# An audio tower with tree feed-forward on one core: the weighing of levels shared out, leaf numbers kept in registers, transposes and residual adds moved

## The chip, the cores and the metric

One core of one Trainium2 chip. The time is that of the kernel on the device, in microseconds; the figure for a kernel is the median of its runs. Beside the plain runs there is one profiled execution, whose own time is given with its span.

## What is computed

Four sequences of 750 rows of 128 features go through a convolution with signs of the inputs and weights (3 taps, 64 features, 748 tokens a sequence), an attention in which only the diagonal of the weights is used, and a tree feed-forward. The change touches the last part only:

```python
h = layernorm(h2)
current = 0
for i in range(8):                       # a path from the root to a leaf level
    score = h . w1s[current] + b1s[current]
    weight_i = gelu(abs(score))
    t_i = h @ w2s[current] + b2s[current]
    out += weight_i * t_i
    current = 2 * current + (score > 0) + 1
result = h2 + out
```

Each of the 2992 tokens so uses eight 64 x 64 matrices, one on each level, chosen by its own path; 128 nodes stand on the last level (the "leaves").

## The kernel before, in words

The part behind 363 us of the profile is the feed-forward. Tokens have been sorted by leaf: every leaf has a fixed group of 32 slots (the static part, 4096 slots in 32 tiles of 128), and tokens that find no room there go to overflow groups of 32 slots, which belong to one leaf each. How many overflow groups there are is known only at run time (`nact`); up to 96 are provided for, in sections of 4 tiles (16 groups) that run only under `If(groups > ...)`. For these inputs three sections are live, 12 tiles and 48 groups. GpSimd scatters the tokens' rows into DRAM (`own_slots`, L646), SP reads them back four tiles at a time into a ring of six (`load_rows`, L433), with two parts per row: the normalised features (with a one for the bias) and the residual `h2`, and the token number.

For every section of four tiles TensorE transposes the rows (`xs_T`, L995) into PSUM tile Z[0], and ScalarE copies them to SBUF (`xs_copy`, L1248, ring of three). The weight tables lie in SBUF with 65 columns a node, the last one w1, so that a product gives both `t_i` and the score. Level 0 to 3, 4 to 5, 6 and 7 are multiplied separately:

- A static tile (`tile_products`, L1016 to L1023) has fixed nodes: one product of 260 columns (4 levels) and one of 130 (2 levels) for 128 slots, two of 65 for 64 slots each, four of 65 for 32 slots each. Its result fills one of three pairs of PSUM banks (`y_bank`): the four upper levels in one bank, the four lower in the other.
- An overflow group (`overflow_products`, L1051 to L1057) has four products for 32 slots (260, 130, 65 and 65 columns) whose weights start at an address that TensorE's queue works out from a register. The leaf numbers, 7 bits each, are packed in pairs in `lami`; `load_leaves` (L1030) brings two registers, for the four groups of the next tile, between the second and the third group. For the even group of a pair each address is a shift, a mask, a multiplication and an addition, for the odd one the mask is not needed. Each group has a pair of banks of its own, and ScalarE copies it to 32 partitions of `yv` in SBUF (L1276).

Behind the products the work of a tile is a chain: ScalarE takes Abs of the eight scores (L1255) and their Gelu (L1257) to `gw`; VectorE multiplies the 8 x 64 outputs by the eight weights into `wy`, a ring of two (`weigh`, L1626), sums the eight levels into `yo`, a ring of twelve (`sum_levels`, L1634), and adds the residual (`add_residual`, L1640); GpSimd scatters the rows to the output with an indirect DMA (`rows_out`, L717). In the static part VectorE's order is weigh k, add the residual of k - 1, sum k. The order within each engine is written out by hand; semaphores tie them: TensorE reuses a pair of banks when `s_wy` says it is weighed (`bank_ready`), VectorE reuses a slot of `yo` when its transfer has landed (`s_outr`), and SP refills a slot of the rows' ring when the four tiles in it are written out. `s_goff` says that the leaf numbers and `nact` are ready.

## Time and profile before

| what | value |
|---|---|
| median of 3 runs | 499.88 us (499.46 to 502.1) |
| the profiled execution | 497.14 us, span 495.4 us |
| busy: PE, DVE, ACT, POOL | 362.6, 353.8, 297.0, 266.6 us |
| static stage, first to last weighing | 368.0 to 421.3 us |
| overflow stage, first product to last copy | 420.5 to 483.65 us |

Times in the views count from the span's start. PE is TensorE's matmul stream, PEld its weight loads, PEldq and POOLq the queues that feed the engines (register operations are not counted as busy), DVE VectorE, ACT ScalarE, POOL GpSimd. A row of the timeline merges neighbouring instructions of one kind ("x2"); in brackets stands how long the engine was idle before, and what it is held to have waited for. In the view by form a row ends with busy time, mean ns of one, and idle time before. The program names are tiles that share memory: `va` holds `xs`, `wy` and `yv`, `pre` holds `yo`, `pool_a` and `w` the weight tables, `qk` the transposed rows.

### The profile page before, as it was taken

How to read it: one execution, taken by the hardware profiler on the slowest of the kernel's cores; microseconds unless marked ns; L12 is line 12 of the kernel's file. 1: busy time of each engine (PE TensorE's matmuls, PEld its weight loads, DVE VectorE, ACT ScalarE, POOL GpSimd, SP SyncE). 2: the span in 40 equal slices, each digit the busy share in tenths (PEclk: the TensorE clock that was granted, in tenths of full speed). 3: DMA queues.
4: the chain of work that ended last, by engine and by line, in shares of the span. 5: the costliest groups of instructions: out<-in, count | busy, mean ns of one | idle time of the engine just before them, and what ended most of it. 6: DMA issues, size and time to landing. Idle time of an engine off the chain costs nothing.

```text
span 495.4 us, 8210 instructions
## 1 busy us (share of the span) xinstructions
PE 362.6 (73%) x2578; PEld 246.1 (50%) x2578; DVE 353.8 (71%) x619; ACT 297.0 (60%) x691; POOL 266.6 (54%) x354
## 2 busy tenths in 40 slices
PE   1158997767998897878987798834069887778880
PEld 1145665545555554456644475522057665545550
DVE  0558869897988888988889979776129999433341
ACT  1357987799789986777976658561013332544551
POOL 4324687885686846855896617417506555321111
PEclk9988989999999999898998989855569999999997
DMA  4443541339969722312441200197151220000000
GB/s 95 120 104 84 125 101 41 93 78 226 202 146 156 162 53 63 93 33 63 110 109 27 69 1 11 38 133 99 32 132 35 56 54 10 6 7 4 7 3 7
DMA packets 58424, 36.99 MB, mean 75 GB/s; under 512 B 31645, under 2 KB 57079, under 8 KB 58378
## 3 DMA queue, kind: packets, MB, share of 16 engines
q1 hardware_dynamic: 54250, 33.55, 33.6%
q0 software_dynamic: 3328, 2.36, 1.9%
q10 hardware_dynamic: 800, 0.49, 0.5%
q8 instruction: 26, 0.43, 0.4%
q14 instruction: 20, 0.16, 0.1%
HBM read 11.15 MB, written 7.50 MB: 38 GB/s over the span
## 4 chain that ended last, share of the span: by engine, by line
DVE 39%; PE 27%; ACT 15%; issue 11%; DMA 5%; POOL 1%; SPq 1%; DVEq 0%; POOLq 0%; ACTq 0%
DVE nm L1367 12%; ACT Z L1183 8%; PE Z L914 8%; DVE pre L1634 6%; PE Z L1051 5%; DVE va L1626 4%; DMA pre<-in_x 3%; DVE va L1396 2%; PE Z L1053 2%; ACT q L1125 2%; PE Z L1057 2%; DVE pre L1463 1%; ACT k L1125 1%; ACT va L1276 1%; PE Z L1055 1%
## 5 line engine op out<-in xcount | busy, mean ns | idle before, releaser
L1367 DVE TENSOR_REDUCE nm<-Z 125x1 f32<-125x748 f32 x192 | 175.4, 932 | 38.9 <-PE Z L914 33.2
L1183 ACT ACTIVATE Z<-Z,nm 125x748 f32<-125x748 f32 x192 | 166.1, 870 | 61.5 <-DVE nm L1367 61.2
L914 PE MATMUL Z<-pool_a 128*125 128x512 f16 (+1 forms) x768 | 164.5, 342 | 27.3 <-ACT Z L1183 23.7
L914 PEld LDWEIGHTS Z<-pool_a 128*125 128x125 f16 x768 | 88.7, 141 | 71.6 <-ACT Z L1183 45.6
L717 POOL DMA_INDIRECT out<-pre,va x44 | 42.7, 971 | 87.8 <-DVE pre L1640 78.3
L1634 DVE TENSOR_REDUCE pre<-va 128x64 f32<-128x512 f32 x44 | 45.1, 1025 | 1.3
L1276 ACT COPY va<-Z 32x520 f32<-32x520 f32 x48 | 27.9, 580 | 30.3 <-PE Z L1057 30.1
L781 PE MATMUL Z<-xhT,wq 128*128 128x249 f16 (+1 forms) x192 | 33.4, 295 | 10.5 <-DVEq L1377 9.2
L1183 ACT ACTIVATION_READ_ACCUMULATOR Z<-Z,nm 125x1 f32 x192 | 41.1, 214 | 0.0
L1051 PE MATMUL Z<-pool_a,qk 128*32 x96 | 29.6, 390 | 14.1 <-ACT va L1276 8.7
L646 POOL DMA_INDIRECT sorted_rows<-xrow,slot x24 | 30.4, 1266 | 15.3 <-DVE slot L1519 8.7
L1626 DVE TENSOR_TENSOR va<-va,gw 128x512 f32<-128x512 f32 x12 | 8.3, 691 | 38.6 <-ACT gw L1257 38.6
L614 POOL TENSOR_TENSOR va<-va 125x256 f32<-125x256 f32 (+2 forms) x54 | 29.5, 547 | 10.2 <-DVE va L1396 7.1
L1626 DVE TENSOR_TENSOR va<-Z,gw 128x512 f32<-128x512 f32 x32 | 21.7, 679 | 18.6 <-ACT gw L1257 18.4
L590 POOL TENSOR_TENSOR pool_a<-q,pool_a 128x748 f16<-128x748 f32 x15 | 24.6, 1643 | 10.2 <-DVE pool_a L1324 9.1
L781 PEld LDWEIGHTS Z<-xhT,wq 128*128 128x128 f16 x192 | 19.2, 106 | 21.1 <-DVEq L1377 13.4
L588 POOL CAST pool_a<-q 128x748 f16<-128x748 f32 x14 | 11.3, 806 | 32.2 <-ACT q L1125 32.2
L793 PEld LDWEIGHTS Z<-sel,qk 128*125 128x125 f32 x192 | 25.4, 194 | 6.0 <-DVEq L1416 1.1
L598 POOL TENSOR_TENSOR qk<-q,k 128x748 f32<-128x748 f32 x16 | 28.3, 1772 | 0.0
L1255 ACT ACTIVATE gw<-Z 128x8 f32<-128x8 f32 x32 | 5.7, 177 | 35.3 <-PE Z L1023 33.7
L793 PE MATMUL Z<-sel,qk 128*125 128x2 f32 x192 | 25.2, 236 | 1.4 <-DVEq L1416 0.9
L1016 PE MATMUL Z<-pool_a,qk 128*128 128x260 f32 x64 | 23.1, 444 | 4.1 <-DVE va L1626 4.1
(237 smaller groups left out, 620.9 us busy)
## 6 DMA issues: line engine op xcount, KB each, us to landing
pool_a<-pool_a SPq DMA_DIRECT2D x64, 187.0 KB, 3.3
pool_a<-pool_a SPq DMA_DIRECT2D x64, 93.5 KB, 2.2
sorted_rows<-zrow SPq DMA_DIRECT2D x1, 3640.0 KB, 22.1
va<-sorted_rows SPq DMA_DIRECT2D x11, 260.0 KB, 3.4
w<-in_L_ffn_w2s SPq DMA_DIRECT2D x1, 2048.0 KB, 16.6
pre<-in_x SPq DMA_DIRECT2D x4, 375.0 KB
pool_a<-in_L_ffn_w2s SPq DMA_DIRECT2D x1, 1024.0 KB
out<-pre,va POOLq DMA_INDIRECT x44, 2.1
```

What stands on the lines that cost most here:

```text
L614: link(gp.tensor_tensor(pw[:, 0:n], pw[:, 0:n], pw[:, n:2 * n], ALU.add))
L646: gp.indirect_dma_start(rows, bass.IndirectOffsetOnAxis(slots[0:XP, t:t + 1].bitcast(u32), 0), xrow[0:XP, t, :], None, bounds_check=SLOTS - 1,
L717: gp.indirect_dma_start(outf, bass.IndirectOffsetOnAxis(ids.bitcast(u32), 0), yo[:, k % NO, :], None, bounds_check=T - 1, oob_is_err=False ...
L781: last = mm(z[:, PSUM_AT[c] % 512:PSUM_AT[c] % 512 + CLASS_N[c]], wq[:, a, g * H * D + j * P:g * H * D + (j + 1) * P], xhT[:, r0:r0 + CLAS ...
L793: last = mm(z[0:XP, t:t + NT + 1:NT], qk[:, w % 3, KST[t]:KST[t] + XP], sel[:], start=True, stop=True)
L914: last = mm(z[0:XP, c0:c1], kst[:, u % 3, a, hd, KST[t]:KST[t] + XP], qst[:, u % 3, hd, c0:c1], start=(a == 0), stop=(a == 1))
L1051: mm(y[:, 0:4 * E1], xg, wlow[:, bass.ds(node(g, 4) * (4 * E1) + T03 * E1, 4 * E1)], start=True, stop=True)
L1183: sc_.activation(z, z, ACT.Exp, bias=nm[0:XP, u % 4, i:i + 1], accum_out=sm[0:XP, u % 4, i:i + 1]).then_inc(s_exp, 1)
L1276: sc_.copy(yv[g * G:(g + 1) * G, k % 2], y_bank(banks(k) + g)[0:G]).then_inc(s_yv, 1)
L1367: v.tensor_reduce(nm[0:XP, u % 4, i:i + 1], Z[n % 3][0:XP, 0:N], X, ALU.max, negate=True).then_inc(s_max, 1)
L1626: v.tensor_tensor(wy[:, k % 2].rearrange("p (h l o) -> p h l o", h=2, o=D), y[:, :, :, 0:D], gw[:, k % 4].rearrange("p (h l) -> p h l", h= ...
L1634: v.tensor_reduce(yo[:, k % NO, :], wy[:, k % 2].rearrange("p (l o) -> p o l", o=D), X, ALU.add).then_inc(s_sl, 1)
```

## The change

Six edits, all in the feed-forward.

1. The static tiles' weighing is split: ScalarE multiplies the four upper levels, with four scaled Copy activations of 64 columns out of PSUM (`weigh_first`), VectorE the four lower ones in one operation of half the size. A bank pair is free, and the sum may start, when both have reported (`s_wa` beside `s_wy`). Overflow tiles are weighed as before.
2. The residual add goes from VectorE to GpSimd, in `rows_out`, ahead of the indirect DMA, for all tiles.
3. The leaf numbers are packed four to a 28-bit word (`lam4`, two more small VectorE operations ahead of `s_goff`), one word a tile. The words of the first 16 overflow tiles are loaded into registers of TensorE ahead of the first transposes; only tiles beyond these load in the loop.
4. In an overflow group the leaf is cut out of its word once and kept in a register (`snap`); the four addresses are worked out from it with a shift, a multiplication and an addition.
5. Transposes and their copy run one section ahead in the overflow too: the first section's beside tile 28, the next one's behind the second tile of each section.
6. SP loads nine sections ahead of its wait for `s_goff` rather than eight, and one section ahead in the loop.

```diff
@@ -161,6 +161,7 @@
...
+        lam4 = sb("lam4", [1, OVG // 4], i32)
...
@@ -179,6 +180,8 @@
         E = [Z[3][:, 0:512], Z[3][:, 512:1024]]
 
         NY = 3
+        AW = 4
+        EARLY = 16
 
         def y_bank(n):
 
@@ -432,13 +435,13 @@
                         sp.wait_ge(s_outr[t % NO], 16 * (t // NO + 1))
                 sp.dma_start(xs[:, k % NX], rv[:, 4 * k:4 * k + 4, :]).then_inc(s_xsr[k % NX], 16)
 
-            for k in range(ST_TILES // 4):
+            for k in range(ST_TILES // 4 + 1):
                 load_rows(k)
             sp.wait_ge(s_goff, 1)
             groups = sp.value_load(nact[0:1, 0:1], min_val=0, max_val=OVG)
-            for k in range(ST_TILES // 4, F_TILES // 4):
+            for k in range(ST_TILES // 4, F_TILES // 4 - 1):
                 with sp.If(groups > 4 * (4 * k - ST_TILES)):
-                    load_rows(k)
+                    load_rows(k + 1)
 
             for k in range(ST_TILES - NO, ST_TILES):
                 sp.wait_ge(s_outr[k % NO], 16 * (k // NO + 1))
@@ -712,6 +715,9 @@
             groups = pool.value_load(nact[0:1, 0:1], min_val=0, max_val=OVG)
 
             def rows_out(k):
+                pool.wait_ge(s_sl, k + 1)
+                o = yo[:, k % NO, :]
+                gp.tensor_tensor(o, o, xs[:, (k // 4) % NX, k % 4, C_H:C_ID], ALU.add).then_inc(s_yo, 1)
                 pool.wait_ge(s_yo, k + 1)
                 ids = xs[:, (k // 4) % NX, k % 4, C_ID:C_ID + 1]
                 gp.indirect_dma_start(outf, bass.IndirectOffsetOnAxis(ids.bitcast(u32), 0), yo[:, k % NO, :], None,
@@ -1006,6 +1012,7 @@
                     pe.wait_ge(s_yv, n - NY - ST_TILES + 1)
                 elif n >= NY:
                     pe.wait_ge(s_wy, n - NY + 1)
+                    pe.wait_ge(s_wa, n - NY + 1)
 
             def tile_products(k):
 
@@ -1027,50 +1034,42 @@
             def load_leaves(k):
 
                 kk = k - ST_TILES
-                return [nc.tensor.value_load(lami[0:1, 2 * kk + i:2 * kk + i + 1], min_val=0,
-                                             max_val=LEAVES * LEAVES - 1) for i in range(2)]
-
-            def overflow_products(k, pairs):
-
-                following = None
-
-                def node(g, sh):
-
-                    if g % 2:
-                        return pairs[g // 2] >> (7 + sh)
-                    return (pairs[g // 2] >> sh) & (LEAVES - 1 >> sh)
+                return nc.tensor.value_load(lam4[0:1, kk:kk + 1], min_val=0, max_val=LEAVES ** 4 - 1)
+
+            def overflow_products(k, leaves):
 
                 tile_ready(k)
                 xk = xsT[:, k // 4 % 3, (k % 4) * P:(k % 4 + 1) * P]
                 for g in range(4):
-                    if g == 2 and k % 4 < 3:
-                        following = load_leaves(k + 1)
                     bank_ready(banks(k) + g)
                     y = Z[1 + (banks(k) + g) % NY][0:G, :]
                     xg = xk[:, G * g:G * (g + 1)]
-                    mm(y[:, 0:4 * E1], xg, wlow[:, bass.ds(node(g, 4) * (4 * E1) + T03 * E1, 4 * E1)],
+                    own = leaves >> 7 * g if g else leaves
+                    leaf = nc.tensor.snap(own & LEAVES - 1 if g < 3 else own)
+                    mm(y[:, 0:4 * E1], xg, wlow[:, bass.ds((leaf >> 4) * (4 * E1) + T03 * E1, 4 * E1)],
                        start=True, stop=True)
-                    mm(y[:, 512:512 + 2 * E1], xg, wlow[:, bass.ds(node(g, 2) * (2 * E1) + T45 * E1, 2 * E1)],
+                    mm(y[:, 512:512 + 2 * E1], xg, wlow[:, bass.ds((leaf >> 2) * (2 * E1) + T45 * E1, 2 * E1)],
                        start=True, stop=True)
-                    mm(y[:, 512 + 2 * E1:512 + 3 * E1], xg, wlow[:, bass.ds(node(g, 1) * E1 + T6 * E1, E1)],
+                    mm(y[:, 512 + 2 * E1:512 + 3 * E1], xg, wlow[:, bass.ds((leaf >> 1) * E1 + T6 * E1, E1)],
                        start=True, stop=True)
-                    mm(y[:, 512 + 3 * E1:512 + 4 * E1], xg, w7all[:, bass.ds(node(g, 0) * E1, E1)],
+                    mm(y[:, 512 + 3 * E1:512 + 4 * E1], xg, w7all[:, bass.ds(leaf * E1, E1)],
                        start=True, stop=True).then_inc(s_y, 1)
-                return following
 
             pe.wait_ge(s_goff, 1)
+            early = [load_leaves(k) for k in range(ST_TILES, ST_TILES + EARLY)]
             xs_T(0)
             for k in range(ST_TILES):
-                if k % 4 == 0 and k + 4 < ST_TILES:
+                if k % 4 == 0:
                     xs_T(k // 4 + 1)
                 tile_products(k)
             groups = pe.value_load(nact[0:1, 0:1], min_val=0, max_val=OVG)
             for m in range(ST_TILES // 4, F_TILES // 4):
                 with pe.If(groups > 4 * (4 * m - ST_TILES)):
-                    xs_T(m)
-                    pairs = load_leaves(4 * m)
                     for k in range(4 * m, 4 * m + 4):
-                        pairs = overflow_products(k, pairs)
+                        n = k - ST_TILES
+                        overflow_products(k, early[n] if n < EARLY else load_leaves(k))
+                        if k % 4 == 1 and k + 4 < F_TILES:
+                            xs_T(m + 1)
 
         @block.scalar
         def _(act):
@@ -1256,18 +1255,28 @@
                 act.wait_ge(s_abs, k + 1)
                 sc_.activation(w, w, ACT.Gelu).then_inc(s_gelu, 1)
 
+            def weigh_first(k):
+
+                act.wait_ge(s_gelu, k + 1)
+                if k >= 2:
+                    act.wait_ge(s_sl, k - 1)
+                y = y_bank(k)
+                for n in range(AW):
+                    last = sc_.activation(wy[:, k % 2, n * D:(n + 1) * D], y[:, 0, n, 0:D], ACT.Copy,
+                                          scale=gw[:, k % 4, n:n + 1])
+                last.then_inc(s_wa, 1)
+
             xs_copy(0)
             for k in range(ST_TILES):
-                if k % 4 == 0 and k + 4 < ST_TILES:
+                if k % 4 == 0:
                     xs_copy(k // 4 + 1)
                 act.wait_ge(s_y, k + 1)
                 gates(k, y_bank(k))
+                weigh_first(k)
             act.wait_ge(s_goff, 1)
             groups = act.value_load(nact[0:1, 0:1], min_val=0, max_val=OVG)
             for m in range(ST_TILES // 4, F_TILES // 4):
                 with act.If(groups > 4 * (4 * m - ST_TILES)):
-                    xs_copy(m)
-
                     for k in range(4 * m, 4 * m + 4):
                         if k >= ST_TILES + 2:
                             act.wait_ge(s_wy, k - 1)
@@ -1276,6 +1285,8 @@
                             sc_.copy(yv[g * G:(g + 1) * G, k % 2], y_bank(banks(k) + g)[0:G]).then_inc(s_yv, 1)
                         act.wait_ge(s_yv, 4 * (k - ST_TILES + 1))
                         gates(k, yv[:, k % 2])
+                        if k % 4 == 1 and k + 4 < F_TILES:
+                            xs_copy(m + 1)
 
         @block.vector
         def _(dve):
@@ -1616,35 +1627,33 @@
             link(v.tensor_copy(lamq[:], lz))
             link(v.tensor_scalar(lamq[:], lamq[:], LEAVES - 1, None, ALU.bitwise_and))
             link(v.tensor_copy(lamf[:], lamq[:]))
-            v.scalar_tensor_tensor(lami[:], lamf[:, 1::2], float(LEAVES), lamf[:, 0::2], ALU.mult,
-                                   ALU.add).then_inc(s_goff, 1)
+            link(v.scalar_tensor_tensor(lami[:], lamf[:, 1::2], float(LEAVES), lamf[:, 0::2], ALU.mult, ALU.add))
+            link(v.tensor_scalar(lam4[:], lami[:, 1::2], 14, None, ALU.logical_shift_left))
+            v.tensor_tensor(lam4[:], lam4[:], lami[:, 0::2], ALU.bitwise_or).then_inc(s_goff, 1)
 
 
             def weigh(k):
                 dve.wait_ge(s_gelu, k + 1)
-                y = y_bank(k) if k < ST_TILES else yv[:, k % 2]
-                v.tensor_tensor(wy[:, k % 2].rearrange("p (h l o) -> p h l o", h=2, o=D), y[:, :, :, 0:D],
-                                gw[:, k % 4].rearrange("p (h l) -> p h l", h=2).unsqueeze(3).to_broadcast([P, 2, 4, D]),
-                                ALU.mult).then_inc(s_wy, 1)
+                w = wy[:, k % 2].rearrange("p (h l o) -> p h l o", h=2, o=D)
+                gv = gw[:, k % 4].rearrange("p (h l) -> p h l", h=2).unsqueeze(3).to_broadcast([P, 2, 4, D])
+                if k >= ST_TILES:
+                    v.tensor_tensor(w, yv[:, k % 2, :, :, 0:D], gv, ALU.mult).then_inc(s_wy, 1)
+                    return
+                y = y_bank(k)
+                v.tensor_tensor(w[:, 1], y[:, 1, :, 0:D], gv[:, 1], ALU.mult).then_inc(s_wy, 1)
 
             def sum_levels(k):
                 if k >= NO:
                     dve.wait_ge(s_outr[k % NO], 16 * (k // NO))
                 dve.wait_ge(s_wy, k + 1)
+                if k < ST_TILES:
+                    dve.wait_ge(s_wa, k + 1)
                 v.tensor_reduce(yo[:, k % NO, :], wy[:, k % 2].rearrange("p (l o) -> p o l", o=D), X,
                                 ALU.add).then_inc(s_sl, 1)
 
-            def add_residual(k):
-                dve.wait_ge(s_sl, k + 1)
-                o = yo[:, k % NO, :]
-                v.tensor_tensor(o, o, xs[:, (k // 4) % NX, k % 4, C_H:C_ID], ALU.add).then_inc(s_yo, 1)
-
             for k in range(ST_TILES):
                 weigh(k)
-                if k >= 1:
-                    add_residual(k - 1)
                 sum_levels(k)
-            add_residual(ST_TILES - 1)
             dve.wait_ge(s_goff, 1)
             groups = dve.value_load(nact[0:1, 0:1], min_val=0, max_val=OVG)
             for m in range(ST_TILES // 4, F_TILES // 4):
@@ -1652,7 +1661,6 @@
                     for k in range(4 * m, 4 * m + 4):
                         weigh(k)
                         sum_levels(k)
-                        add_residual(k)
 
 
 _INS = ["x", "L0_tok_kernel", "L0_tok_bias", "L0_tok_beta", "L0_tok_moving_mean", "L0_tok_moving_var",
```

(The declaration of the semaphore `s_wa` is left out.)

## Rows read from the trace of the kernel before

**Rows 1.** Timeline of a static tile (start us, us); last, all weighings by source.

```profile
401.30 1.03 DVE L1634 TENSOR_REDUCE pre<-va 128x64 f32<-128x512 f32 x1
...
402.24 0.68 DVE L1626 TENSOR_TENSOR va<-Z,gw 128x512 f32<-128x512 f32 x1
...
402.76 0.18 ACT L1255 ACTIVATE gw<-Z 128x8 f32<-128x8 f32 x1 [1.32 <-PE Z L1023]
...
402.97 0.21 ACT L1257 ACTIVATE gw<-gw 128x8 f32<-128x8 f32 x1
...
402.98 0.49 PE L1016 MATMUL Z<-pool_a,qk 128*128 128x260 f32 x1 [0.29 <-DVE va L1626]
...
L1626 DVE TENSOR_TENSOR va<-Z,gw x32: 669/678/692, 368.0 to 421.3; 128x512 f32<-128x512 f32 x32
```

**Rows 2.** Timeline of TensorE, two successive tiles early in the static stage.

```profile
373.85 0.71 PE L1016 MATMUL Z<-pool_a,qk 128*128 128x260 f32 x2
...
375.22 0.71 PE L1016 MATMUL Z<-pool_a,qk 128*128 128x260 f32 x2
```

**Rows 3.** Timeline of TensorE, first products of groups; last, that line by source.

```profile
430.05 0.62 PE L1051 MATMUL Z<-pool_a,qk 128*32 x2
...
430.95 0.60 PE L1051 MATMUL Z<-pool_a,qk 128*32 x2
...
431.94 0.62 PE L1051 MATMUL Z<-pool_a,qk 128*32 x2
...
434.08 0.62 PE L1051 MATMUL Z<-pool_a,qk 128*32 x2 [1.07 <-ACT va L1276]
...
L1051 PE MATMUL Z<-pool_a,qk x96: 381/383/402, 420.5 to 482.8; 128*32 x96
```

**Rows 4.** By source, TensorE's queue, 430.6 to 434: ns min/median/max, first, last start.

```profile
L1051 PEldq ALU_OP  x2: 36/36/36, 430.6 to 430.7; - x2
...
L1051 PEldq FUSED_REGOPS  x2: 61/70/80, 431.8 to 434.0; - x2
...
L1030 PEldq TENSOR_LOAD <-lami x2: 296/299/302, 432.5 to 433.1; - x2
...
L1051 PEldq ALU_OP  x2: 36/36/36, 433.8 to 433.9; - x2
```

**Rows 5.** Timeline: leaf numbers on VectorE, first transposes on TensorE.

```profile
349.38 0.23 DVE L1619 SCALAR_TENSOR_TENSOR lami<-lamf 1x48 int32<-1x48 f32 x1
...
363.31 0.87 PE L995 MATMUL Z<-idf,va 128*65 128x128 f32 x3 [14.72 <-DMA va<-sorted_rows]
```

**Rows 6.** ScalarE: three ACTIVATEs in the timeline, then two groups by form.

```profile
27.88 1.19 ACT L1125 ACTIVATE q<-Z,bq 128x249 f32<-128x249 f32 x3 [1.68 <-PE Z L781]
...
L1125 ACT ACTIVATE q<-Z,bq 128x249 f32<-128x249 f32 x32 | 13.2, 470 | 2.6 <-PE Z L781 2.6
...
L1183 ACT ACTIVATE Z<-Z,nm 125x748 f32<-125x748 f32 x192 | 166.1, 870 | 61.5 <-DVE nm L1367 61.2
```

**Rows 7.** VectorE by form: a weighing of 256 elements.

```profile
L1412 DVE TENSOR_TENSOR va<-Z,at 125x256 f32<-125x256 f32 x4 | 1.7, 415 | 0.2 <-DVE va L1412 0.2
```

**Rows 8.** GpSimd: timeline around its shortest interval; an add of 64 elements.

```profile
423.15 0.23 DVE L1640 TENSOR_TENSOR pre<-pre,va 128x64 f32<-128x64 f32 x1
...
424.20 0.97 POOL L717 DMA_INDIRECT out<-pre,va  x1 [0.30 <-issue]
...
L615 POOL TENSOR_TENSOR xrow<-xrow,va 125x64 f32<-125x64 f32 x18 | 5.5, 306 | 1.4
```

**Rows 9.** Timeline of the tail: last copy, weighing, reduction and transfer.

```profile
483.65 0.58 ACT L1276 COPY va<-Z 32x520 f32<-32x520 f32 x1 [0.35 <-PE Z L1057]
...
484.75 0.69 DVE L1626 TENSOR_TENSOR va<-va,gw 128x512 f32<-128x512 f32 x1 [1.72 <-ACT gw L1257]
...
485.54 1.01 DVE L1634 TENSOR_REDUCE pre<-va 128x64 f32<-128x512 f32 x1
...
487.61 0.97 POOL L717 DMA_INDIRECT out<-pre,va  x1 [2.82 <-DVE pre L1640]
```

More of the change, by code:

```diff
@@ L214, in tower @@
             "slots", "ln2_rstd", "w1_columns")]
-        (s_b0, s_bnp, s_bn, s_bq8, s_z7, s_zl, s_abs, s_xp, s_xc, s_y, s_yv, s_wy, s_sl, s_yo) = [sem(n) for n in (
-            "b0_in", "bn_by_feature", "bn_ready", "q_bias_ready", "w7_zeros", "low_zeros", "gate_abs", "xs_T", "xsT_copied", "y_ready", "y_moved", "weighted", "levels_summed", "rows_out")]
+        (s_b0, s_bnp, s_bn, s_bq8, s_z7, s_zl, s_abs, s_xp, s_xc, s_y, s_yv, s_wa, s_wy, s_sl, s_yo) = [sem(n) for n in (
+            "b0_in", "bn_by_feature", "bn_ready", "q_bias_ready", "w7_zeros", "low_zeros", "gate_abs", "xs_T", "xsT_copied", "y_ready", "y_moved", "weighted_by_act", "weighted", "levels_summed", "rows_out")]
         vs, ps_, as_ = sem("vector_step"), sem("pool_step"), sem("scalar_step")
```

## The prediction

> **What bounds the kernel now.** I read the page first (slices and chain), then the stretch behind 363 us by stages, since nothing ahead of it is touched. The feed-forward has two stages, bounded differently.
>
> The static stage, 32 tiles, is paced by VectorE. The 32 weighings start between 368.0 and 421.3 [rows 1], 53.3 us for 31 steps, 1.72 us a tile. The timeline of one tile shows the reduction at 401.30 (1.03 us) and the next weighing 0.94 us later, at 402.24, before the reduction has quite ended: no gap. The other 0.78 us hold the weighing (0.68) and the residual add. TensorE's first product of a later tile starts at 402.98, only after a weighing has freed its bank, and ScalarE has idled 1.32 us before its 0.18 us Abs. TensorE alone is faster: before its banks are all taken it starts a tile every 375.22 - 373.85 = 1.37 us [rows 2]; four transposes per four tiles add about 0.1, so **1.47 us** a tile.
>
> The overflow stage, 12 tiles of 4 groups, goes from 420.5 to 483.6 [rows 3, 9], 63.1 us. The wait view blames ScalarE's copy for TensorE's holes, but the queue records say otherwise. The groups start at 430.05, 430.95, 431.94 and then 434.08 [rows 3]: 0.90, 0.99 and 2.14 us. In that last step the queue runs two register loads, at 432.5 and 433.1, and reaches the next address arithmetic at 433.8 [rows 4]: 1.3 us in which nothing is issued. An even group, whose leaf must be masked out of a pair before each product, takes the queue from 430.6 to 431.8, 1.2 us; an odd one, which needs one fused operation per product, from 431.8 to 432.5, **0.7 us** [rows 4]. So this stage is bound by TensorE's instruction queue, at 5.1 us a tile, while the array needs 0.90 a group, 3.6 a tile.
>
> **Start of the stage.** Sixteen register loads come ahead of the first transposes. One costs 433.1 - 432.5 = 0.6 us [rows 4], sixteen 10 us. The leaf numbers are written at 349.61, and with two such 0.23 us VectorE operations more near 350.1; the loads then end near 360.2. The first transposes wait until 363.31 for the sorted rows' DMA, TensorE idle for 14.72 us [rows 5]. Cost nothing, 3 us to spare; without that cover it would be 10 us. Bounds: 0 to 2 us (loads of 0.8 us each would end at 363). SP's order only gains a ninth row load ahead of its wait; each refill waits for rows written some 17 tiles ahead of its use, so I take 0.
>
> **Static stage, after.**
> - VectorE: half a weighing reads 256 elements; such a one took 0.415 us [rows 7] against 0.68. The add is gone, but it stood between weighing and reduction and hid the write of the first. In the overflow stage, with no such cover, the reduction starts at 485.54, 0.10 us after the weighing's end [rows 9]. So 0.415 + 0.10 + 0.95 = **1.47 us** a tile.
> - ScalarE: four scaled copies of 64 elements. No row has that size. Three ACTIVATEs of 249 elements with a per-partition operand fill 1.19 us, single ones 0.470, so one slot is 0.36; the 748-wide ones take 0.870 [rows 6], a slope of 0.80 ns an element. A slot for 64 is then 0.36 - 185 x 0.0008 = 0.21 us, four 0.85. The ends are 0.10 (only the streaming left) and 0.36 (no gain from the size). With Abs and Gelu, 0.18 + 0.21 + 0.05 for their waits [rows 1], and a quarter of a 0.58 us copy of transposed rows (its size: [rows 9]), ScalarE needs 1.4 us (1.0 to 2.0).
> - TensorE: 1.47 as now. It must see two engines release a bank; the round trip products, gates, copies is about 1.4 + 0.5 + 1.0 = 2.9 us over three banks, 1.0 a tile, and no bound.
> Three engines within 0.07 us of each other will not interleave perfectly: I take 1.50 us. Tile 5 starts at 373.85 [rows 2]; TensorE then ends tile 31 near 373.85 + 26 x 1.47 + 1.37 = 413.4 and, after the section count's load and branch (about 1 us, transposes and their copy being done already), begins the overflow at 414.4 in place of 420.5: **-6.0 us** (0 to -6.5).
> The Trainium skill (ScalarE: Activation LUTs, What ACT_TABLE_LOAD costs) gives 186 ns + 0.833 ns an element, 93 ns for a pointer operand and 93 ns of overlap. By it a slot is 0.24 us and ScalarE needs 1.52 a tile; the stage would be ScalarE's and the gain 1.5 us smaller. The rows above agree within 0.03 us.
>
> **Overflow stage, after.** All live leaves are in registers: the loads go, and every product has one fused operation, as in today's odd groups. Ahead of a group stand one or two operations for the shift and the mask; from the even groups, (1.2 - 0.7) / 7 = 0.07 us each. Queue: 4 x 0.7 + 6 x 0.07 = 3.2 us a tile, 3.6 if each value also costs a move. The array's 0.90 x 4 = 3.6 takes over; a little friction gives 0.93 a group, 12 x 3.72 = 44.6 us. Today's 12 x 5.12 = 61.4 leaves 1.7 us for the crossings of sections; transposes inside the stream (three sets, one of them for a section that is not live) and branches cost about the same. **-16.8 us** (-10 to -18).
> ScalarE needs 4 x 0.58 + 0.6 = 2.9 us a tile and VectorE 1.9, both under 3.7, and are hidden.
>
> **Tail and GpSimd.** The add of 125x64 took 0.306 us [rows 8] against VectorE's 0.23, plus one more hand-over: **+0.15 us** (0 to 0.5) behind the last tile, on the path. But every tile now makes GpSimd wait for its own add before it may start its transfer. The transfer begins 0.82 us after the event it waits for (add ended 423.38, transfer 424.20) although only 0.30 us after the previous one [rows 8]; half of that preparation is now exposed. Period: 0.31 + 0.05 + 0.80 + 0.97 = **2.12 us** (1.65 to 2.3) against 1.5 of the others. Its first transfer starts near 371.0 (weighing at 368.0, 0.68 + 0.10 + 1.03 to the reduction's end, then the add and the preparation), and it falls behind through the static stage, by 19 us at tile 31. Twelve output slots take this, barely: the transfer of tile 19 starts at 371.0 + 19 x 2.12 = 411.3, and tile 31, which reuses its slot, reduces near 415.5; above 2.3 us a tile VectorE would start to wait here. In the overflow GpSimd catches up: its last transfer could start at 371.0 + 43 x 2.12 = 462.2, while TensorE ends at 414.4 + 46.4 = 460.8 and the last transfer is due 4.2 us later, 465.0 (today 4.0: 487.61 behind 483.6 [rows 9]). Hidden, by 2.8 us.
>
> **Sum.** -6.0 - 16.8 + 0.15 = -22.6 us. The profiled execution took 497.14 us (span 495.4), so 474.5; the median of the runs, 499.88, lies 2.7 above that execution, so **477.3 us**.
>
> **Rivals.**
> - Forecast: TensorE's stream bounds the overflow, all three engines the static stage. 0.62.
> - The queue stays the bound: a kept register is itself made by more operations, or each product keeps a shift beside its fused one, 0.7 + 5 x 0.07 = 1.05 us a group. For it: each group gets operations that no odd group has now. Against it: masks go from four a group to one. 48 x 1.05 = 50.4, 6 us later: 483. Or a load per tile stays because the registers are not kept, 12 x 0.6 = 7 us: 484.5. 0.12 together.
> - ScalarE bounds the static stage, at 1.7 us or more with slots of 0.28: no gain there, 483.5; at the upper end, 2.0 us a tile, it loses 9 us and gives 492. 0.10.
> - GpSimd becomes the end. Above 2.19 us a tile it decides; at 2.4 its last transfer starts at 474.2, 9 us late: 486.5. 0.11.
> - The same on the other side: GpSimd's period above (487.61 - 371.0) / 43 = 2.71 us makes the kernel slower, at 3.0 by 12 us, 512. This needs an add of 0.9 us in place of 0.31; the 748-wide ones take longer than that, none of 64 does. 0.05, with other losses.
>
> **How the numbers follow.** A measurement of this kernel tells about 0.5%, 2.5 us. Range: 473 (1.47 us a tile, 0.90 a group, and the profiled execution as the base) to 486.5, which takes in the queue case and most of the ScalarE and GpSimd cases; a fifth is left out. Faster by over 0.5%: 0.92, within: 0.03, slower: 0.05.
>
> **What would show it.** Right: group starts 0.9 us apart with no 2.1 us step; sixteen register loads between 350 and 361 and the first transposes still at 363; weighings 1.5 us apart; GpSimd without idle time until late in the overflow, transfers 2.1 us apart; the last product near 461. Wrong: loads between tiles; TensorE waiting for ScalarE's release in the static stage; VectorE waiting for written output slots; a chain that ends in GpSimd rather than in TensorE; an ACT_TABLE_LOAD behind the gates.

## The result and the profile after

| | before | after |
|---|---|---|
| median of the runs | 500.0 us (499.46 to 502.1, 4 runs) | 476.0 us (474.18 to 477.09, 4 runs) |
| the profiled execution | 497.14 us, span 495.4 | 475.4 us, span 473.5 |
| busy: PE, DVE, ACT, POOL | 362.6, 353.8, 297.0, 266.6 us | 359.0, 340.6, 324.1, 283.9 us |
| first to last static weighing | 53.3 us | 369.2 to 416.8: 47.6 us |
| first overflow product to the last one's end | 420.5 to 483.6 | 414.6 to 460.6 |

The ratio is 0.951 (0.947 to 0.955): 4.9% faster. The forecast was 477.3 us. Executions more than 1.5% above the fastest of their kernel are left out of this and all later ratios, not out of the medians and ranges.

**The static stage**, one tile in the timeline of the changed kernel:

```profile
396.00 0.42 DVE L1643 TENSOR_TENSOR va<-Z,gw 128x256 f32<-128x256 f32 x1
...
396.01 0.99 POOL L723 DMA_INDIRECT out<-pre,va  x1 [0.79 <-POOL pre L720]
...
396.26 0.93 ACT L1265 ACTIVATE va<-Z,gw 128x64 f32<-128x64 f32 x4
396.50 1.04 DVE L1651 TENSOR_REDUCE pre<-va 128x64 f32<-128x512 f32 x1
...
397.03 0.31 POOL L720 TENSOR_TENSOR pre<-pre,va 128x64 f32<-128x64 f32 x1
...
397.47 0.41 DVE L1643 TENSOR_TENSOR va<-Z,gw 128x256 f32<-128x256 f32 x1
...
398.13 0.99 POOL L723 DMA_INDIRECT out<-pre,va  x1 [0.79 <-POOL pre L720]
```

Weighings stand 1.47 us apart here, and over tiles 5 to 28, where they stood 1.72 apart [rows 1]; over all 31 steps it is 47.6 / 31 = 1.54, because the first steps are longer (2.18, 1.98 and, a little later, 1.76 and 2.00 us). The weighing takes 0.42 us, the sum follows 0.08 us behind it and takes 1.04. ScalarE's four copies fill 0.93 us (the view by line gives 316 ns for a single one, so (0.93 - 0.316) / 3 = 0.205 a slot). They are those of the next tile, so this sum does not wait for them. (Six of the 32 sums do wait for ScalarE's copies, 2.7 us in all, three of them in the first six tiles.) GpSimd starts a transfer every 2.12 us, 0.79 us idle in each turn: it falls behind from here on, as forecast.

**The overflow stage**, the first product of successive groups in TensorE's timeline, then line 1049 by source (ns min/median/max, first and last start):

```profile
416.11 0.62 PE L1049 MATMUL Z<-pool_a,qk 128*32 x2 [0.42 <-DVE va L1643]
...
417.55 0.62 PE L1049 MATMUL Z<-pool_a,qk 128*32 x2 [0.37 <-DVE va L1643]
...
419.34 0.60 PE L1049 MATMUL Z<-pool_a,qk 128*32 x2
...
421.11 0.60 PE L1049 MATMUL Z<-pool_a,qk 128*32 x2
...
422.00 0.60 PE L1049 MATMUL Z<-pool_a,qk 128*32 x2
```

```profile
L1049 PE MATMUL Z<-pool_a,qk x96: 381/382/407, 414.6 to 459.8; 128*32 x96
L1049 PEldq ALU_OP  x60: 32/36/42, 414.4 to 457.8; - x60
L1049 PEldq FUSED_REGOPS  x48: 77/77/109, 414.5 to 458.7; - x48
```

A group takes 0.89 us (419.34 to 421.11 are two, 422.00 the next), the third of each tile too, where [rows 3] had a step of 2.14; only where transposes stand in between, once in each section, it is 1.56. Two holes, 0.42 and 0.37 us, stand at the start, where the last static tiles' banks are not yet weighed. The queue has one fused operation per group for this product, and 60 plain ones for 48 groups are the shifts and masks. No load is left in the loop; they stand ahead of the first transposes, by source and in the timeline:

```profile
L1037 PEldq TENSOR_LOAD <-lam x16: 293/303/488, 351.4 to 361.6; - x16
```

```profile
364.39 0.91 PE L1001 MATMUL Z<-idf,va 128*65 128x128 f32 x3 [14.64 <-DMA va<-sorted_rows]
```

They end 2.1 us ahead of the rows' DMA, at 0.68 us each. The DMA is 1.1 us later than in [rows 5]; so is everything ahead of it (the operation of [rows 5] on the leaf numbers starts at 350.54 rather than 349.38), in work that the change does not touch.

**The end.** First the timeline of the changed kernel's tail on VectorE and GpSimd, then the queues' last instructions by source, before and after. DRAIN is what each queue runs last; COMPARE_BRANCH is TensorE's skip over a section that is not live.

```profile
461.75 0.69 DVE L1640 TENSOR_TENSOR va<-va,gw 128x512 f32<-128x512 f32 x1 [1.68 <-ACT gw L1256]
462.02 1.28 POOL L723 DMA_INDIRECT out<-pre,va  x1 [0.79 <-POOL pre L720]
462.55 1.01 DVE L1651 TENSOR_REDUCE pre<-va 128x64 f32<-128x512 f32 x1
463.34 0.31 POOL L720 TENSOR_TENSOR pre<-pre,va 128x64 f32<-128x64 f32 x1
464.44 0.99 POOL L723 DMA_INDIRECT out<-pre,va  x1 [0.80 <-POOL pre L720]
465.46 0.33 POOL L720 TENSOR_TENSOR pre<-pre,va 128x64 f32<-128x64 f32 x1
466.58 0.99 POOL L723 DMA_INDIRECT out<-pre,va  x1 [0.79 <-POOL pre L720]
```

```profile
L1069 PEldq COMPARE_BRANCH  x3: 3242/3930/4623, 483.1 to 491.8; - x3
...
L70 POOLq DRAIN  x1: 6385/6385/6385, 487.9 to 487.9; - x1
...
L70 PEldq DRAIN  x1: 73/73/73, 495.1 to 495.1; - x1
```

```profile
L1067 PEldq COMPARE_BRANCH  x3: 385/3422/4692, 459.3 to 464.5; - x3
...
L70 POOLq DRAIN  x1: 6361/6361/6361, 466.8 to 466.8; - x1
L70 PEldq DRAIN  x1: 66/66/66, 468.0 to 468.0; - x1
```

Before, GpSimd's drain ended at 487.9 + 6.4 = 494.3, but TensorE's three skips (3.9, 4.6 and 3.2 us) held its own drain until 495.1: TensorE's skips ended the kernel, 0.8 us behind what GpSimd alone would have given. After, the skips are over at 468.0 and GpSimd's drain ends at 466.8 + 6.36 = 473.2, against a span of 473.5. VectorE's last sum is done at 463.56, and by GpSimd's own add and preparation (0.34 + 0.85) its transfer was due at 464.75; it starts at 466.58. **GpSimd is 1.8 us late**, and so ends the kernel.

The bill, of spans: everything up to the first weighing +1.1; first weighing to first overflow product 52.4 to 45.5, **-6.9**; the overflow's products 63.2 to 46.0, **-17.2**; from the last product's end to the span's end 11.8 to 12.9, **+1.1**. Sum -21.9, from 495.4 to 473.5.

### The profile page after: what moved, and what is told of

Same layout as the page of the kernel before. It is cut to its first block, busy times and chain, and to the rows that moved or that the text cites. A ratio compares the mean times of both kernels' runs of the same rounds, so it can differ in the third digit from the quotient of the medians.

```text
span 473.5 us, 8286 instructions
## 1 busy us (share of the span) xinstructions
PE 359.0 (76%) x2582; PEld 249.7 (53%) x2582; DVE 340.6 (72%) x577; ACT 324.1 (68%) x820; POOL 283.9 (60%) x398
## 4 chain that ended last, share of the span: by engine, by line
DVE 25%; PE 21%; issue 17%; ACT 16%; POOL 13%; DMA 5%; SPq 1%; ACTq 0%; POOLq 0%; DVEq 0%
DVE nm L1378 11%; PE Z L920 10%; ACT Z L1182 10%; POOL out L723 9%; POOL pre L720 3%; DVE va L1407 2%; ACT q L1124 2%; DMA va<-in_L_attn_Wqkv 2%; ACT k L1124 2%; DVE pre L1474 2%; PE Z L840 1%; PE Z L799 1%; PE Z L787 1%; DVE pre L1489 1%; DMA par<-in_L_tok_moving_var 1%
## 5 line engine op out<-in xcount | busy, mean ns | idle before, releaser
L920 PE MATMUL Z<-pool_a 128*125 128x512 f16 (+1 forms) x768 | 167.8, 347 | 23.9 <-ACT Z L1182 19.9
L920 PEld LDWEIGHTS Z<-pool_a 128*125 128x125 f16 x768 | 91.0, 144 | 68.1 <-ACT Z L1182 40.8
L723 POOL DMA_INDIRECT out<-pre,va x44 | 44.7, 1016 | 35.0 <-POOL pre L720 35.0
L1651 DVE TENSOR_REDUCE pre<-va 128x64 f32<-128x512 f32 x44 | 45.7, 1038 | 5.9 <-ACT va L1265 2.7
L787 PE MATMUL Z<-xhT,wq 128*128 128x249 f16 (+1 forms) x192 | 34.6, 303 | 11.7 <-DVEq L1388 10.4
L1265 ACT ACTIVATE va<-Z,gw 128x64 f32<-128x64 f32 x128 | 29.8, 316 | 1.1
L1247 ACT COPY qk<-Z 65x512 f32<-65x512 f32 x12 | 7.0, 581 | 28.5 <-PE Z L1001 28.3
L1643 DVE TENSOR_TENSOR va<-Z,gw 128x256 f32<-128x256 f32 x32 | 13.3, 414 | 18.3 <-ACT gw L1256 18.2
```

What stands on the lines that cost most here:

```text
L723: gp.indirect_dma_start(outf, bass.IndirectOffsetOnAxis(ids.bitcast(u32), 0), yo[:, k % NO, :], None, bounds_check=T - 1, oob_is_err=False ...
L787: last = mm(z[:, PSUM_AT[c] % 512:PSUM_AT[c] % 512 + CLASS_N[c]], wq[:, a, g * H * D + j * P:g * H * D + (j + 1) * P], xhT[:, r0:r0 + CLAS ...
L920: last = mm(z[0:XP, c0:c1], kst[:, u % 3, a, hd, KST[t]:KST[t] + XP], qst[:, u % 3, hd, c0:c1], start=(a == 0), stop=(a == 1))
L1265: last = sc_.activation(wy[:, k % 2, n * D:(n + 1) * D], y[:, 0, n, 0:D], ACT.Copy, scale=gw[:, k % 4, n:n + 1])
L1651: v.tensor_reduce(yo[:, k % NO, :], wy[:, k % 2].rearrange("p (l o) -> p o l", o=D), X, ALU.add).then_inc(s_sl, 1)
```

## Experiments

Every kernel ran beside the one before on the same chip. "Ratio" is to that one, with its 95% interval; Each edit starts from the changed kernel unless another is named.

### The residual adds

First the overflow's adds alone are put back on VectorE.

```diff
 def rows_out(k):
+    if k < ST_TILES:
         pool.wait_ge(s_sl, k + 1)
...
         pool.wait_ge(s_yo, k + 1)
+    else:
+        pool.wait_ge(s_oa, k - ST_TILES + 1)
...
 for k in range(4 * m, 4 * m + 4):
     weigh(k)
     sum_levels(k)
+    add_residual(k)
```

> Residual add of the 12 overflow tiles back on VectorE, that of the 32 static tiles stays on GpSimd. Theory (GpSimd ends the kernel: it waits for its own add and then for the 0.8 us preparation of each transfer, 2.13 us a tile, and still works off its debt when the last tile comes): in the overflow its transfers now follow each other at 1.3 us, the debt is gone by mid-stage, the last transfer starts 1.1 us behind the end of the last reduction instead of 3.0, and the time is 1.8 us shorter, 474.2, ratio near 0.947. Rival (the tail's extra microsecond is not GpSimd's): no change, 476. On the slow records (adds of 0.67, transfers of 1.3 us beside VectorE's weighings of overflow tiles): if only two reads of SBUF collide, the slow transfers stay away together with the adds' collisions only if they were caused by them; if writing descriptors collides as well, transfers of 1.2 to 1.3 us remain.

Measured: 473.35 us, 0.9535 (0.9448 to 0.9623), span 470.7. GpSimd's timeline in the overflow:

```profile
439.93 0.99 POOL L726 DMA_INDIRECT out<-pre,va  x1 [0.79 <-POOL pre L721]
441.22 0.97 POOL L726 DMA_INDIRECT out<-pre,va  x1 [0.30 <-issue]
442.50 0.98 POOL L726 DMA_INDIRECT out<-pre,va  x1 [0.30 <-issue]
```

Without an add between them transfers stand 1.28 us apart, the debt of the static stage is gone by 452, and the last transfer (463.8) follows its sum and its add by 1.1 us. From the last product's end to the span's end it takes 10.9 us in place of 12.9. GpSimd's lateness is what the tail lost.

Next, GpSimd keeps all adds, but in the static part it adds tile k + 1 before it sends tile k, so that preparing a transfer no longer waits for an add just issued.

```diff
+add_rows(0)
 for k in range(ST_TILES):
+    if k + 1 < ST_TILES:
+        add_rows(k + 1)
     rows_out(k)
```

> In the static part GpSimd adds tile k+1 before it starts the transfer of tile k, so that its wait for the own add and the preparation of the transfer lie beside other work; overflow unchanged. Theory (0.5 of the 0.8 us of preparation was exposed by the self-wait): the static period of GpSimd falls from 2.13 to 1.6 or 1.65 us, the debt at tile 31 from 20 to about 5 us, the last transfer starts 1.2 us behind the last reduction, 474.2, ratio near 0.947. Rival (the preparation cannot overlap with an add): period stays at 2.1, time at 476.

Measured: 474.68 us, 0.9552 (0.9476 to 0.9628), span 471.9. In GpSimd's timeline:

```profile
394.91 0.99 POOL L727 DMA_INDIRECT out<-pre,va  x1 [0.17 <-issue]
395.93 0.33 POOL L720 TENSOR_TENSOR pre<-pre,va 128x64 f32<-128x64 f32 x1
396.43 0.99 POOL L727 DMA_INDIRECT out<-pre,va  x1 [0.17 <-issue]
```

The same two instructions take 1.52 us a tile in place of 2.12, and GpSimd keeps up with the other engines; the last transfer starts 1.2 us behind the end of its sum, and the tail is 11.0 us. So 0.6 of the 2.12 us was preparation behind the add, and it is order, not work, that puts GpSimd behind.

Last, all adds go back to VectorE, in the static part where they stood before (`weigh(k); add_residual(k - 1); sum_levels(k)`), with the split kept. This kernel is called "adds on VectorE" below.

> All residual adds back on VectorE, in the old places; everything else as in the changed kernel. Theory (VectorE is within 0.02 us of being the static stage's bound): the add costs its 0.19 us slot but takes back the 0.10 us of wait between weighing and reduction, so a tile needs 1.47 + 0.09 to 0.19 = 1.56 to 1.66 us, the overflow starts 3 to 6 us later, GpSimd's debt is gone (minus 1.8): 477 to 480.5. Rival (ScalarE or TensorE has been the bound with slack on VectorE): the static stage stays at 1.53 us a tile and the time falls by 1.8 to 474.2.

Measured: 471.46 us, 0.9488 (0.9416 to 0.956), span 470.6: the expectation of my theory, 477 to 480.5, was wrong. VectorE's timeline:

```profile
398.24 0.42 DVE L1640 TENSOR_TENSOR va<-Z,gw 128x256 f32<-128x256 f32 x1
398.57 0.22 DVE L1654 TENSOR_TENSOR pre<-pre,va 128x64 f32<-128x64 f32 x1
398.75 1.03 DVE L1648 TENSOR_REDUCE pre<-va 128x64 f32<-128x512 f32 x1
...
399.70 0.41 DVE L1640 TENSOR_TENSOR va<-Z,gw 128x256 f32<-128x256 f32 x1
```

The step is 1.46 us, as without the add. From the weighing's start to the sum's start it takes 0.51 us with the add and 0.50 without (396.00 to 396.50 above). The add of 0.22 us starts before the weighing's record has ended and covers the time in which the sum had to wait for the weighing's output anyway: on VectorE it was **free**, and its move gained nothing. Over tiles 5 to 28 both kernels need 1.47 us a tile; all static weighings take 46.8 us with the adds and 47.6 without, a difference that lies in the first steps.

The same kernel was timed again, on another chip.

> The version with all residual adds on VectorE once more, against the kernel before, with more rounds. Theory (the move of the adds to GpSimd costs 2 to 3 us and wins nothing): ratio 0.944 to 0.950, below the changed kernel's 0.9509.

Measured: 472.44 us (468.2 to 481.4, 6 runs), 0.944 (0.9375 to 0.9505), against 0.951 (0.947 to 0.955) for the change. The intervals overlap by a little. What carries the verdict is the part of the trace that differs: last product's end to span's end, 10.8 us in the first profile of this kernel and 10.9 in the second (462.6 to 473.5), 12.9 in the changed one. It is 10.8 to 11.0 in all eight profiles of kernels that keep the split and whose GpSimd is on time for the last tile.

### The split of the weighing

```diff
-                    pe.wait_ge(s_wa, n - NY + 1)
...
-                weigh_first(k)
...
+                y = y_bank(k) if k < ST_TILES else yv[:, k % 2]
+                v.tensor_tensor(w, y[:, :, :, 0:D], gv, ALU.mult).then_inc(s_wy, 1)
```

> The static weighing wholly on VectorE again (8 levels, ScalarE only gates), adds stay on GpSimd. Theory: 0.68 + 0.10 (wait for its own write, no longer covered by the add) + 0.95 = 1.73 us a tile, as slow as the kernel before although VectorE has lost an instruction; static stage 6 us longer, GpSimd's debt smaller by 6 us so that it ends on time (minus 1.8): 480 to 481, ratio near 0.961. Rival (the write's latency costs nothing): 1.63 us a tile, 477.5.

Measured: 479.64 us, 0.9649 (0.9519 to 0.9779), span 475.5. VectorE's timeline:

```profile
397.80 0.68 DVE L1638 TENSOR_TENSOR va<-Z,gw 128x512 f32<-128x512 f32 x1
...
398.57 1.03 DVE L1644 TENSOR_REDUCE pre<-va 128x64 f32<-128x512 f32 x1
399.52 0.68 DVE L1638 TENSOR_TENSOR va<-Z,gw 128x512 f32<-128x512 f32 x1
```

1.72 us a tile again although VectorE has no add. From the first weighing to the first overflow product it takes 50.6 us instead of 45.5: the split is worth **5.2 us** (5.7 against 44.9 us in the kernel that adds a tile ahead, whose weighing is the same), the rest of the static stage's 6.9 are transposes and crossing, below. At the end of the kernel less of it arrives: without the split GpSimd has the time to catch up, the last transfer starts 1.2 us behind the end of its sum, and the tail is 11.0 us in place of 12.9.

Which engine bounds the stage now? Three kernels take work away in tiles 2 to 31. In the first ScalarE leaves out one of its four levels, in the second VectorE weighs two of its four, in the third both; the results lack those levels' terms.

```diff
-                for n in range(AW):
+                for n in range(AW if k < 2 else AW - 1):
...
-                v.tensor_tensor(w[:, 1], y[:, 1, :, 0:D], gv[:, 1], ALU.mult).then_inc(s_wy, 1)
+                n = 4 if k < 2 else 2
+                v.tensor_tensor(w[:, 1, 0:n], y[:, 1, 0:n, 0:D], gv[:, 1, 0:n], ALU.mult).then_inc(s_wy, 1)
```

> The changed kernel, but from tile 2 on ScalarE weighs three of its four levels of a static tile; the fourth is left out of the computation (the sum reads what the ring held before). It takes 0.21 us a tile from ScalarE alone. Theory (the static stage, 1.46 us a tile in steady state, is bound by TensorE's own 1.37 + 0.1): weighings still span 47 to 47.6 us. Rival A (ScalarE bounds it): 4 us shorter or more.

> The changed kernel, but from tile 2 on VectorE weighs two of its four levels of a static tile; the other two are left out of the computation. It takes 0.13 us a tile from VectorE alone. Theory (TensorE bounds): weighings still span 46.5 to 47.6 us, and waits for ScalarE's weighing or Gelu appear ahead of VectorE's operations. Rival B (VectorE bounds, by its wait between weighing and reduction): 4 us shorter.

> Both of these at once: ScalarE weighs three levels, VectorE two, the remaining three are left out. Theory (TensorE's floor): the stage is no shorter than 31 x 1.47 = 45.6 us, so at most 2 us below now. Rival C (two engines tie and only both together free the stage): 4 us or more.

One execution each: 484.72, 477.53 and 477.15 us. Their totals say little. The first began the stage 9 us late, with TensorE's mean granted clock at 0.875 rather than 0.90, in work that the edit does not touch; and all three end, like the changed kernel, with a GpSimd that is behind. From the first weighing to the last product's end the changed kernel and these three take 91.5, 90.5, 90.6 and 89.7 us, but to the end of the span 104.3, 104.4, 104.5 and 104.6: what the other engines gain, GpSimd's lateness takes back. The weighings of each, by source, tell:

```profile
L1643 DVE TENSOR_TENSOR va<-Z,gw x32: 408/414/425, 378.2 to 424.9; 128x256 f32<-128x256 f32 x32
```

```profile
L1644 DVE TENSOR_TENSOR va<-Z,gw x32: 273/280/426, 370.5 to 417.2; 128x128 f32<-128x128 f32 x30, 128x256 f32<-128x256 f32 x2
```

```profile
L1644 DVE TENSOR_TENSOR va<-Z,gw x32: 274/280/424, 370.6 to 416.4; 128x128 f32<-128x128 f32 x30, 128x256 f32<-128x256 f32 x2
```

46.7, 46.7 and 45.8 us, where the change has 47.6 and "adds on VectorE" 46.8. With 0.2 us less on ScalarE and 0.13 less on VectorE in every tile (6 and 4 us in all) the stage gets at most 1.8 us shorter, most of it in the first steps: over tiles 5 to 28 the mean step is 1.471, 1.460 and 1.461 us, against 1.474. Its floor is TensorE's 31 x 1.47 = 45.6 us: **TensorE bounds it**. VectorE ties with it, however. In the changed kernel nearly all later steps are 1.46 us, VectorE's own time for weighing, gap and sum; with VectorE relieved they become 1.37, 1.37, 1.37 and 1.77, TensorE's three tiles without transposes and one with them, of the same mean.

### The leaf numbers

These start from "adds on VectorE". First, no word is loaded early: each overflow tile loads its own in the loop (`EARLY = 16` becomes `EARLY = 0`).

> From here on the base is the version with all residual adds on VectorE (471.5 us), in which GpSimd hides nothing. One part undone: no leaf word is loaded early, each overflow tile loads its own word in the loop. Theory (TensorE's queue runs only a few tenths ahead of the array): a load holds the queue for 0.6 us; the queue's own work is about 3.2 us a tile against 3.56 of the array, so 0.25 to 0.6 us a tile shows, group starts 1.2 to 1.5 us apart once a tile: 3 to 7 us more, 474.5 to 478.5. Rival (the loads would be hidden behind queued products, and the mask alone was the cost): no change.

Measured: 474.99 us, 0.9539 (0.9472 to 0.9607), span 473.6. TensorE's timeline, first weight loads and products of groups across a tile's end:

```profile
430.87 0.60 PE L1046 MATMUL Z<-pool_a,qk 128*32 x2
432.02 0.14 PEld L1046 LDWEIGHTS Z<-pool_a,qk 128*32 128x32 f32 x2 [0.27 <-issue]
432.03 0.62 PE L1046 MATMUL Z<-pool_a,qk 128*32 x2
```

This step is 1.16 us in place of 0.89 (the longest without transposes is 1.21), and the stage from its first to its last first-product takes 45.5 us in place of 44.6, 0.9 us more. The first tile's load also stands ahead of the first product: that starts 0.7 us ahead of the last static weighing, not 1.5. From the last static weighing to the last product's end it takes 45.7 us, in place of 43.9 in both profiles of the base: **1.8 us** for twelve loads, below the theory's 3 to 7 and above the rival's nothing. (The spans differ by 3.0 us, of which 1.5 lie ahead of the first weighing.) A load holds the queue for 0.67 us and costs 0.15 us a tile: most of it fits into what the queue has to spare over the array.

Second, the register is not kept (`snap` taken away).

> Same base. The leaf is not kept in a register: each of the four addresses is worked out from the tile's word with its own shift and mask. Theory: three groups of four cost the queue 1.0 to 1.2 us instead of 0.7 to 0.85, above the array's 0.89, so the overflow needs 0.1 to 0.3 us more a group, 5 to 12 us in all: 476 to 483. Rival (the kept register changes nothing, or the compiler works the value out per product anyway): no change.

Measured: 472.48 us, 0.9476 (0.9385 to 0.9568). The queue's records of line 1046 by source:

```profile
L1046 PEldq ALU_OP  x60: 32/36/42, 411.0 to 453.9; - x60
L1046 PEldq FUSED_REGOPS  x48: 77/77/109, 411.1 to 454.7; - x48
```

They are those of the changed kernel, in number and in length, and the stage is 44.6 us. Since the masked leaf is one shared expression, it is worked out once with or without the call. Keeping it in a register by name does nothing. So the expected 5 to 12 us were never put to the test: in both notations the mask is made once per group, and no run makes it for each product.

Third, the sixteen early loads are made twice.

```diff
+            for k in range(ST_TILES, ST_TILES + EARLY):
+                load_leaves(k)
             early = [load_leaves(k) for k in range(ST_TILES, ST_TILES + EARLY)]
```

> Same base. The sixteen early loads are done twice. They run from 351.4 to 362.2 now, 0.68 us each, and the first transposes wait for the rows' DMA until 364.4. Theory (the loads are hidden with 2 us to spare): sixteen more cost 10.9 us, of which 2.1 are still covered, so everything behind moves by 8.8 us: span 479.4 against 470.6. Rival (the queue can load while it waits for a semaphore elsewhere, or loads overlap each other): under 3 us.

One execution: 478.63 us, span 476.8. Loads by source, first transposes in the timeline:

```profile
L1034 PEldq TENSOR_LOAD <-lam x32: 295/301/489, 350.3 to 371.0; - x32
```

```profile
371.67 1.97 PE L998 MATMUL Z<-idf,va 128*65 128x128 f32 x8 [23.00 <-issue]
```

The transposes come at 371.67 rather than 364.3, no longer behind a DMA ("issue") but behind the queue. 32 loads take (371.0 - 350.3) / 31 = 0.67 us each. The 16 early loads are hidden by the rows' DMA and by nothing else; the second 16 cost 7.4 us there, of which the span shows 6.2. The theory had 8.8 us. Here the loads begin 1.0 us earlier than in the base (350.3 rather than 351.3), by work ahead of them that the edit does not touch; with that added the shift is 8.4.

### Transposes a section ahead

```diff
-            for k in range(ST_TILES // 4 + 1):
+            for k in range(ST_TILES // 4):
...
-                if k % 4 == 0:
+                if k % 4 == 0 and k + 4 < ST_TILES:
...
+                    xs_T(m)
...
-                        if k % 4 == 1 and k + 4 < F_TILES:
-                            xs_T(m + 1)
```

and the same for the copies and SP's loads, on "adds on VectorE".

> Same base. Transposes, their copies and the row loads of the overflow sections are no longer a section ahead but stand at the head of their section. Theory: each of three sections starts with transposes, 0.65 us, a copy, 0.58, and two hand-overs in which TensorE has nothing else, 1.3 us more than now; minus 0.6 for the section that is not live: 3 to 4 us more, 474.5 to 475.5. Rival (the queue had time to spare there, or the bank waits of the first groups cover it): under 1 us.

Measured: 477.29 us, 0.9583 (0.9528 to 0.9638), span 474.9. The waits ahead of line 1046, by source, and one crossing in TensorE's timeline:

```profile
  ACT qk L1243: 4.3, 3
```

```profile
432.57 0.58 ACT L1243 COPY qk<-Z 65x512 f32<-65x512 f32 x1
...
433.42 0.62 PE L1046 MATMUL Z<-pool_a,qk 128*32 x2 [1.30 <-ACT qk L1243]
```

Three sections, three stops for ScalarE's copy, 4.3 us together. First weighing to first overflow product takes 47.1 us in place of 45.3, the overflow's first products 46.2 in place of 44.6: **3.4 us**, within the forecast's 3 to 4. The total lies above its forecast; the spans differ by 4.3 us, of which 0.9 lie ahead of the first weighing.

## Why the prediction was right, and where it was not

**The total was right mainly by its steps, and in part by luck.** The overflow was to begin at 414.4 and TensorE to end at 460.8; they came at 414.6 and 460.6. The static stage was to gain 6.0 us (measured 6.9, counted from its own first weighing), the overflow 16.8 (17.2), and 1.47 us a tile and 0.93 a group became 1.47 and 0.89. Luck is that the start of the overflow came out within 0.2 us: everything ahead of the stage ran 1.1 us late, and the "about 1 us" for the section count's load and branch did not appear, because TensorE's first overflow product follows the last static one without a gap (414.63 behind a product of 414.46). The prediction also took 1.50 us a tile for friction and then reckoned with 1.47; with 1.50 the overflow would begin at 415.2 and the total be 478.1. The profiled execution was to take 474.5 us and took 475.4; the 2.7 us put on top for the median were 0.6. A slot of ScalarE's copies was to take 0.21 us from the slope in [rows 6], and takes 0.205. The Trainium skill (ScalarE: Activation LUTs, What ACT_TABLE_LOAD costs) gives, by an estimate from its figures, 186 + 93 + 0.833 x 64 = 332 ns for a single copy and, less 93 ns of overlap, 240 for a slot; measured are 316 and 205. Single costs agree within 5%, the overlap is larger (0.11 us) than its 93 ns. The stage that ScalarE would bound at 1.52 us a tile did not come.

**"Hidden, by 2.8 us" failed.** GpSimd's period was to be 2.12 us to the end. It was 2.12 to 2.13 in the static part, but (465.46 - 371.3) / 43 = 2.19 over all its adds, the very value from which the rival said it decides. Three things ate the margin: the first transfer starts at 372.5 instead of 371.0, most of it the 1.1 us from ahead of the stage; 0.01 us a tile; and in the overflow seven of GpSimd's instructions grow. These are neighbours in the changed kernel's timeline:

```profile
450.42 0.69 DVE L1640 TENSOR_TENSOR va<-va,gw 128x512 f32<-128x512 f32 x1 [1.72 <-ACT gw L1256]
450.65 1.32 POOL L723 DMA_INDIRECT out<-pre,va  x1 [0.79 <-POOL pre L720]
...
453.96 0.69 DVE L1640 TENSOR_TENSOR va<-va,gw 128x512 f32<-128x512 f32 x1 [1.71 <-ACT gw L1256]
454.14 0.66 POOL L720 TENSOR_TENSOR pre<-pre,va 128x64 f32<-128x64 f32 x1
```

Four transfers (1.21 to 1.32 us, else 0.99) and three adds (0.66 to 0.69, else 0.31 to 0.34) each start while VectorE runs an overflow weighing, which reads both its inputs from SBUF; together they cost 2.2 us. Started first, GpSimd is not stretched and the weighing is instead (up to 0.81 us, and 0.88 in the kernel with the overflow's adds on VectorE). Beside the static weighings, which read PSUM, no instruction of GpSimd is that long. The Trainium skill (SBUF — State Buffer, Who interferes with whom) says that a VectorE instruction with two SBUF inputs contends with a GpSimd instruction that reads SBUF, that contention is an exclusive lock, and that the order of issue decides who is blocked. The trace agrees on who is stretched, but overlaps of 0.35 to 0.52 us cost 0.22 to 0.36, not all of it. The same section of the Trainium skill infers that the generation of descriptors is not held up by such an operation. Here the transfers are stretched; they also read their row numbers from SBUF, and no run separates the two. The prediction took GpSimd's durations from stretches where the two did not meet. The case "GpSimd becomes the end" so came true at its edge, not at 2.4 us a tile: 1.8 us late rather than 9. It was priced as a rival and named among the signs of being wrong ("a chain that ends in GpSimd"); the total hid it, because it was small. With the static adds ahead, or all adds on VectorE, the longest transfer is 1.01 us; with only the overflow's adds moved there are still some of 1.14, 1.26 and 1.32 on the way, which do not matter because GpSimd catches up by 452.

**"The add is gone, but it stood between weighing and reduction and hid the write of the first" was right, and not carried to its end.** It was used to price the new step, and not to ask what the old add had cost. It costs nothing on VectorE with either weighing: with the full one a tile takes 1.72 us before, with the add, and 1.72 in the kernel without the split, which has none. So moving it bought GpSimd's lateness for no gain. The expectation of that experiment still charged 0.1 to 0.2 us a tile for it.

**The attribution inside the 16.8 us was off.** No run measures the queue's own time a tile, put at 3.2 to 3.6 us against the array's 3.6; that a load of 0.67 us costs 0.15 a tile fits the lower end. "The loads go" was the smaller part: once masks are made once a group, one load per tile costs 1.8 us in all. How the rest of the 17.2 us divides between the second load, the masks and their hold-up of the queue was not tried. "Crossings of sections cost about the same" hid a term: with transposes ahead they cost 3.4 us less, some 1.6 of it in the overflow and 1.8 at its start, where the prediction had counted them as "being done already" and given no price.

**Early loads:** 0.68 us each in place of 0.6, 2.1 us to spare in place of 3. The second set shows that nothing else covers them.

**The tail, "+0.15 us",** became +1.1. Of the last product's end to the last transfer it is 4.0 to 5.96, the 1.8 us of lateness and 0.15 of the slower add and its hand-over. But some 0.8 came back, because the end before was not set by the output at all: TensorE's skips over three sections that are not live had held it. The prediction's chain stopped at the last transfer and did not look at what the queues did behind it.

**What stays open:** why a skip takes TensorE's queue 3 to 4.7 us (0.38 in one case, 0.05 on GpSimd), what masks for each product would cost, and whether in the collisions it is GpSimd's reads, its writes or its access as such that VectorE holds up; none of these was tried. "Adds on VectorE" and the change were never timed side by side, so their difference rests on the tail in the traces.

## What to carry to other kernels

Before work is moved off an engine, look at what it covers there: here a 0.22 us add lay in the time that VectorE waits for its own output, and cost nothing where it stood. An engine that runs behind is hidden only as long as its debt, its period times all tiles, is paid back before the last one; take that period from a stretch where its neighbours do what they will do then, and put the next tile's independent work between an operation and what waits for it. And read the queues behind the last busy instruction, for they may be what ends the kernel.

## What the runs showed of the hardware

- A VectorE operation with both inputs in SBUF and a GpSimd add or indirect transfer hold each other up: the later one of the two is longer by up to 0.4 us (GpSimd add 0.31 to 0.71 us, indirect transfer 0.99 to 1.32; VectorE weighing 0.69 to 0.88).
- An indirect transfer on GpSimd starts 1.1 us behind the start of an add that it waits for (0.79 idle), 0.30 us behind a transfer's end, and 0.17 us behind an unrelated add. It takes 0.97 to 0.99 us.
- A register load on TensorE's queue costs 0.67 us; one per tile of 3.6 us cost 1.8 us over twelve tiles, 0.15 each; thirty-two in a row took 21 us.
- GpSimd's last instruction, a drain, took 6.35 to 6.39 us in every kernel shown, so the last transfer it issues starts at least 6.8 us ahead of the end of the span.
- Skipping a section that is not live takes TensorE's queue 3.2 to 4.6 us in the kernel before, 0.4 to 4.7 in the changed one, and 0.05 us on GpSimd.
